# Turned weights split by TensorE, codes in fewer operations, and second counts taken early

## What is computed

```python
h = jnp.maximum(_layernorm(x, axis=-1), 0.0)
# layer 0: for each edge (s, d): relu(concat(h[s], h[d]) @ W0.T + b0), summed at s
x = x + _L0_gnn_ref(h, edge_index_t, 1250, L0_gnn_W, L0_gnn_b)
h = jnp.maximum(_layernorm(x, axis=-1), 0.0)
# layer 1: (h @ W1.T)[s] * edge_weight, summed at d, then out >= 0 ? out : alpha * out
x = x + _L1_gnn_ref(h, edge_index, edge_weight, 1250, L1_gnn_W, L1_gnn_alpha)
```

## Time and profile before

| | us |
|---|---|
| median of three runs | 1033.83 (1033.64 to 1035.51) |
| the profiled execution | 1024.19 |
| its span, first to last instruction | 1022.5 |
| TensorE, VectorE, ScalarE, GpSimd busy | 962.6, 889.8, 776.2, 663.5 |

### The profile page before, as it was taken

One profiled execution on the slowest core, in us unless ns is written; L12 is line 12 of the kernel. 1 busy time (PEld: TensorE's weight loads), 2 busy tenths in 40 slices (PEclk: granted clock), 3 DMA queues, 4 the chain that ended last, 5 costly groups with the idle time before them and its releaser, 6 DMA issues.

```text
span 1022.5 us, 20099 instructions
## 1 busy us (share of the span) xinstructions
PE 962.6 (94%) x4679; PEld 769.9 (75%) x4680; DVE 889.8 (87%) x1753; ACT 776.2 (76%) x1648; POOL 663.5 (65%) x942
## 2 busy tenths in 40 slices
PE   5389999999989999999999999999999999989998
PEld 4177778776758887888887888888888787878776
DVE  7989999898769999999999999999999788883444
ACT  6668788787868888888888888888888777764210
POOL 3788878786567777777777777777777755540000
PEclk9999999899979999999999999999999999999999
DMA  8000000000111111111111111111111000010011
GB/s 219 1 4 2 3 3 3 4 2 3 17 53 43 44 41 40 41 44 42 44 40 40 43 42 42 43 40 40 43 42 45 30 27 29 30 42 1 20 41 41
DMA packets 34384, 35.09 MB, mean 34 GB/s; under 512 B 6129, under 2 KB 30556, under 8 KB 34337
## 3 DMA queue, kind: packets, MB, share of 16 engines
q1 hardware_dynamic: 29636, 33.89, 10.8%
q0 software_dynamic: 4416, 0.30, 1.6%
q10 hardware_dynamic: 284, 0.33, 0.1%
HBM read 30.92 MB, written 3.29 MB: 33 GB/s over the span
## 4 chain that ended last, share of the span: by engine, by line
PE 68%; DVE 2%; ACT 1%; issue 0%; POOL 0%; POOLq 0%
PE node_ps L1127 8%; PE edge_ps L1166 8%; PE edge_ps L1172 8%; PE edge_ps L1171 7%; PE edge_ps L1167 7%; PE node_ps L1128 7%; PE m_ps L1138 4%; PE psum L1270 3%; PE psum L1272 3%; PE psum L1271 3%; PE m_ps L1252 1%; PE edge_ps L1230 1%; PE edge_ps L1231 1%; PE edge_ps L1227 1%; PE edge_ps L1222 1%; PE edge_ps L1226 1%
## 5 line engine op out<-in xcount | busy, mean ns | idle before, releaser
L1359 ACT ACTIVATE msg_hi<-edge_ps 128x512 fp32r<-128x512 f32 x332 | 198.0, 596 | 59.3 <-PE edge_ps L1172 59.3
L1083 POOL TENSOR_TENSOR M<-M,pair_w 125x125 f32 x332 | 161.2, 485 | 124.3 <-DVE pair_w L1506 94.6
L1520 DVE SCALAR_TENSOR_TENSOR msg_lo<-edge_ps,msg_hi 128x512 fp32r<-128x512 f32 x332 | 224.2, 684 | 17.1 <-ACT msg_hi L1359 12.3
L409 POOL DMA_INDIRECT edge_table<-fields,row_no x136 | 175.2, 1288 | 54.7 <-issue 46.4
L812 ACT ACTIVATE lane_piece<-hot_lane,fields 125x128 fp32r<-125x128 bf16 x498 | 155.8, 391 | 41.6 <-DVE hot_lane L495 41.4
L698 PE MATMUL psum<-hot_tile,lane_piece 125*128 125x384 f32 x582 | 147.2, 375 | 20.6 <-ACT lane_piece L812 19.5
L1067 POOL TENSOR_TENSOR hot_w<-hot_d,weight_l 128x252 fp32r<-128x252 bf16 x166 | 141.6, 853 | 0.0
L698 PEld LDWEIGHTS psum<-hot_tile,lane_piece 125*128 125x128 f32 x582 | 106.1, 197 | 42.1 <-ACT lane_piece L812 25.9
L1127 PE MATMUL node_ps<-msg_hi,hot_s 128*125 128x512 f32 x332 | 134.8, 406 | 0.0
L1166 PE MATMUL edge_ps<-b_hi,turned_d 125*128 x332 | 132.5, 399 | 0.9 <-ACT turned_d L1343 0.7
L1172 PE MATMUL edge_ps<-a_lo,turned_s 125*128 x332 | 131.5, 396 | 0.0
(11 more groups left out here) (256 smaller groups left out, 2062.6 us busy)
## 6 DMA issues: line engine op xcount, KB each, us to landing
spread<-edge_rows SPq DMA_DIRECT2D x190, 125.0 KB
out_dram<-result SPq DMA_DIRECT2D x10, 224.0 KB
edge_table<-fields,row_no POOLq DMA_INDIRECT x136, 2.6
w_in<-in_L_gnn_W_dram SPq DMA_DIRECT2D x1, 2048.0 KB, 11.7
S<-in_x_dram SPq DMA_DIRECT2D x1, 1792.0 KB
w_in<-in_L_gnn_W_dram SPq DMA_DIRECT2D x1, 1024.0 KB, 5.3
S<-in_x_dram SPq DMA_DIRECT2D x1, 448.0 KB
edge_table<-zeros SPq DMA_DIRECT2D x1, 384.0 KB, 15.5
```

What stands on the lines that cost most here:

```text
L409: pool.indirect_dma_start(table_dram[:, :], bass.IndirectOffsetOnAxis(ap=row_no[:, c:c + 1], axis=0), fields[:, c, 0:TABLE_FIELDS], None). ...
L1083: pool.tensor_tensor(part, part, pair_w[h][:, j, 0, 0:BN], ALU.add).then_inc(m_added, 1)
L1359: act.activation(msg_hi[j][:], edge_ps[j][:], ACT.Relu).then_inc(hi_ready, 1)
L1520: dve.scalar_tensor_tensor(out=msg_lo[j][:], in0=edge_ps[j][:], scalar=0.0, in1=msg_hi[j][:].bitcast(F32), op0=ALU.max, op1=ALU.subtract). ...
```

## The change

TensorE: `turn_w` is now a plain matmul with the identity as moving operand; each group of four opens with `start` and leaves the result to be added to. A new `low_w(i)` subtracts the rounded weights (`minus_ident` times `w0T[0]`) in the same PSUM bank, and ScalarE copies what is left as `w0T[1]`. `w0T_full` and GpSimd's eight subtractions are gone, as is the semaphore `w_full`; `w_low`, `ones_row_r` and `mix_bases` are new. The weights go in four pairs: two ahead of and around the column of bases, two behind the 15 prefixes and ahead of the first column. No transposing stands before the totals any more.

Counts of the second chunk are taken directly behind those of the first, in banks 0 and 2, and copied by ScalarE in two operations after the second pair of weights. VectorE makes the sixth block of `hot` before it waits for the totals, the mix bases before the scan, and leaves `base_up` to ScalarE. The codes are computed on one plane of 330 columns, without the operation over both planes. GpSimd's three `fields` operations wait for the codes instead of the base rows.

The core of the diff (blank lines and most context left out):

```diff
@@ -237,7 +236,10 @@
             HALF = CHUNK // 2
-            count_ps = psum[0:NBLK, 4:6, 0:HALF * NBLK]
+            def count_ps(k):
+                return [psum[0:NBLK, bank, 0:HALF * NBLK] for bank in ((0, 2) if k == 1 else (4, 5))]
             turn_ps = psum[:, 2, 0:KC * BN].rearrange("p (c n) -> p c n", c=KC)
@@ -367,7 +371,7 @@
-                    pool.tensor_copy(ones_r[:], ones[0:2, :]).then_inc(w_lo, 1)
+                    pool.tensor_copy(ones_r[:], ones[0:2, :]).then_inc(ones_row_r, 1)
                     own(pool.memset(all_one, 1.0))
@@ -378,17 +382,12 @@
-                    pool.wait_ge(base_rows, 2)
+                    pool.wait_ge(code_ready, 1)
                     pool.wait_ge(weight_in, 16)
...
                                        ALU.subtract).then_inc(fields_ready, 1)
-                    for i in range(2 * KC):
-                        pool.wait_ge(w_full, i + 1)
-                        pool.tensor_tensor(w0T[1][:, i, :], w0T_full[i][:], w0T[0][:, i, :].bitcast(F32),
-                                           ALU.subtract).then_inc(w_lo, 1)
@@ -542,6 +541,7 @@
                                       by_col[:].unsqueeze(1).to_broadcast(shape), ALU.mult).then_inc(spread_done, 1)
+                    hot_of_block(0, 5)
                     dve.tensor_copy(iota_h[:], iota[:, 0:P])
@@ -581,27 +581,25 @@
                     own(dve.tensor_reduce(counts[:, :, 0], own_base.rearrange("p s d -> p d s"), AX.X, ALU.add))
+                    own(dve.tensor_tensor(own_mix[:], base_p.rearrange("p (s q) k -> p s q k", s=NBLK)[0:NBLK, :, :, 1],
+                                          ident[0:NBLK, 0:NBLK].unsqueeze(2).to_broadcast([NBLK, NBLK, NBP]), ALU.mult))
+                    dve.tensor_reduce(mix_at[:], own_mix.rearrange("p s q -> p q s"), AX.X, ALU.add).then_inc(mix_bases, 1)
                     dve.wait_ge(consts, 5)
                     bases(0)
-                    own(dve.tensor_tensor(own_mix[:], base_p.rearrange("p (s q) k -> p s q k", s=NBLK)[0:NBLK, :, :, 1],
-                                          ident[0:NBLK, 0:NBLK].unsqueeze(2).to_broadcast([NBLK, NBLK, NBP]), ALU.mult))
-                    own(dve.tensor_reduce(mix_at[:], own_mix.rearrange("p s q -> p q s"), AX.X, ALU.add))
-                    dve.tensor_scalar(base_up.rearrange("s (q k) c -> s q (k c)", k=2),
-                                      mix_at[:].unsqueeze(2).to_broadcast([NBLK, NBP, 2 * CHUNK]), -float(MID_TILE), UPPER,
-                                      ALU.add, ALU.mult).then_inc(upper_row, 1)
-                    for s in range(5, NBLK):
+                    for s in range(6, NBLK):
                         hot_of_block(0, s)
-                    own(dve.scalar_tensor_tensor(out=local[:], in0=blk[:], scalar=-float(BN), in1=node_f[:],
+                    upper_bits = local[:, 0, :]
+                    own(dve.scalar_tensor_tensor(out=upper_bits, in0=node_f[:, 0, :], scalar=float(TILE), in1=node_f[:, 1, :],
                                                  op0=ALU.mult, op1=ALU.add))
-                    own(dve.scalar_tensor_tensor(out=local[:, 0, :], in0=local[:, 0, :], scalar=float(TILE),
-                                                 in1=local[:, 1, :], op0=ALU.mult, op1=ALU.add))
-                    own(dve.scalar_tensor_tensor(out=local[:, 0, :], in0=blk[:, 1, :], scalar=-UPPER / 2, in1=local[:, 0, :],
+                    own(dve.scalar_tensor_tensor(out=upper_bits, in0=blk[:, 0, :], scalar=-float(BN * TILE), in1=upper_bits,
                                                  op0=ALU.mult, op1=ALU.add))
-                    own(dve.scalar_tensor_tensor(out=local[:, 0, :], in0=pair_of, scalar=UPPER, in1=local[:, 0, :],
+                    own(dve.scalar_tensor_tensor(out=upper_bits, in0=blk[:, 1, :], scalar=-(UPPER / 2 + BN), in1=upper_bits,
                                                  op0=ALU.mult, op1=ALU.add))
-                    dve.tensor_scalar(fields[:].bitcast(I32)[:, :, CODE_AT], local[:, 0, :], float(SHIFT_S * TILE + 1) - UPPER,
+                    own(dve.scalar_tensor_tensor(out=upper_bits, in0=pair_of, scalar=UPPER, in1=upper_bits,
+                                                 op0=ALU.mult, op1=ALU.add))
+                    dve.tensor_scalar(fields[:].bitcast(I32)[:, :, CODE_AT], upper_bits, float(SHIFT_S * TILE + 1) - UPPER,
                                       65536.0, ALU.add, ALU.mult).then_inc(code_ready, 1)
@@ -664,11 +662,11 @@
                         for c in cols:
-                            if c == 0 and k > 0:
+                            if c == 0 and k > 1:
...
                             at = k * CHUNK + c
-                            mm = pe.matmul(count_ps[:, c // HALF, (c % HALF) * NBLK:(c % HALF + 1) * NBLK],
+                            mm = pe.matmul(count_ps(k)[c // HALF][:, (c % HALF) * NBLK:(c % HALF + 1) * NBLK],
                                            dig_s[:, :, at], dig_d[:, :, at], start=True, stop=True)
@@ -700,11 +698,25 @@
                     def turn_w(i):
                         if i >= 2:
-                            pe.wait_ge(w_full, i - 1)
+                            pe.wait_ge(w_lo, i - 1)
                         for o in range(KC):
-                            mm = pe.transpose(psum[:, 6 + i % 2, o * P:(o + 1) * P], w_in[:, o, i * P:(i + 1) * P], ident[:])
+                            mm = pe.matmul(psum[:, 6 + i % 2, o * P:(o + 1) * P], w_in[:, o, i * P:(i + 1) * P], ident[:],
+                                           start=(o == 0), stop=(o == KC - 1), skip_group_check=True)
                         mm.then_inc(w_ps, 1)
+                    def low_w(i):
+                        pe.wait_ge(w_hi, i + 1)
+                        pe.matmul(psum[:, 6 + i % 2, :], minus_ident[:], w0T[0][:, i, :], start=False, stop=True,
+                                  skip_group_check=True).then_inc(w_low, 1)
+                    def weights(pair):
+                        for i in (2 * pair, 2 * pair + 1):
+                            turn_w(i)
+                        for i in (2 * pair, 2 * pair + 1):
+                            low_w(i)
@@ -719,7 +731,8 @@
                             if b == 0 and m == 0:
-                                pe.wait_ge(w_lo, 2 * KC + 1)
+                                pe.wait_ge(w_lo, 2 * KC)
+                                pe.wait_ge(ones_row_r, 1)
                                 pe.wait_ge(bias_in, 32)
@@ -746,20 +759,26 @@
                     mm.then_inc(hist_done, 1)
-                    pe.wait_ge(w_loaded, 16)
-                    turn_w(0)
                     pe.wait_ge(spread_done, 1)
...
                     count(0, range(CHUNK))
-                    for i in range(1, 2 * KC):
-                        turn_w(i)
+                    count(1, range(CHUNK))
+                    pe.wait_ge(w_loaded, 16)
+                    pe.wait_ge(act_own, 2)
+                    weights(0)
...
                     pe.matmul(base_col_ps, tile_base[0:1, :], ones[0:1, 0:1], start=True, stop=True).then_inc(base_col, 1)
+                    weights(1)
                     for g in range(NPICK):
                         prefix(0, g)
+                    weights(2)
+                    weights(3)
                     pe.wait_ge(base_out, 1)
+                    pe.wait_ge(count_out, 2)
@@ -775,8 +794,6 @@
                                         low(b, m)
-                            if k == 0 and i < 3:
-                                count(1, range(CHUNK // 3 * i, CHUNK // 3 * (i + 1)))
                             part = i - last + COUNT_BACK
@@ -798,8 +815,14 @@
                             act.wait_ge(carried, k)
+                        if k == 1:
+                            for h in range(2):
+                                ins = act.copy(counts[:, :, 1 + h * HALF:1 + (h + 1) * HALF],
+                                               count_ps(k)[h].rearrange("s (c d) -> s d c", d=NBLK))
+                            ins.then_inc(count_out, 1)
+                            return
                         act.copy(counts[:, :, 1:CHUNK + 1].rearrange("s d (h c) -> s d h c", h=2),
-                                 count_ps.rearrange("s h (c d) -> s d h c", d=NBLK)).then_inc(count_out, 1)
+                                 psum[0:NBLK, 4:6, 0:HALF * NBLK].rearrange("s h (c d) -> s d h c", d=NBLK)).then_inc(count_out, 1)
@@ -849,31 +872,39 @@
-                    def turned_weights(i):
-                        act.wait_ge(w_ps, i + 1)
-                        act.copy(w0T[0][:, i, :], psum[:, 6 + i % 2, :])
-                        act.copy(w0T_full[i][:], psum[:, 6 + i % 2, :]).then_inc(w_full, 1)
+                    def turned_weights(pair):
+                        for i in (2 * pair, 2 * pair + 1):
+                            act.wait_ge(w_ps, i + 1)
+                            act.copy(w0T[0][:, i, :], psum[:, 6 + i % 2, :]).then_inc(w_hi, 1)
+                        for i in (2 * pair, 2 * pair + 1):
```

(16 more changed lines are left out.)

5 lines of the change are left out of this document (3 added, 2 removed).

## The result

| | kernel before | changed kernel |
|---|---|---|
| median, 17 runs each | 1032.28 (1027.84 to 1036.9) | 1023.22 (1015.37 to 1031.86) |
| profiled execution | 1024.19 | 1019.37 |
| its span | 1022.5 | 1017.6 |

The ratio is 0.9912, with a 95% interval of 0.989 to 0.9934: **9.1 us faster, 6.8 to 11.4**. More runs also moved the median of before, from 1033.83 to 1032.28. The medians are of all 17 runs each; three of the changed kernel (1031.62, 1031.70 and 1031.86), over 1.5% above its fastest, are counted as slow and left out of the ratio, and without them its median would be 1021.73.

A forecast was written before the change was run, and what follows sets the result against it. VectorE's own path was taken to set the stretch before the edge stage. Low clock 3.9 + 3.1 - 1.7 = 5.3 us, high 5.0 + 3.1 = 8.1; 6.5 taken: 1033.83 - 6.5 = 1027.3 us, range 1024.2 to 1031.7.

The forecast's parts named there:

- Earlier start of the bases: VectorE ahead of the codes: totals free of transposes, line 552 at 15.6 instead of 15.87, last hot block about 25.6 instead of 27.39.
- The codes: VectorE just before the picks: 2.5 us instead of 6.3 with GpSimd quiet, so picks could begin at 28.05.
- A turn: One weight turned on TensorE by plain fp32 matmuls: 8 x 0.23 = 1.82 us.
- TensorE ahead of the picks: Counts and two pairs of turns precede the first prefix: picks at about 29.8, 3.9 us won, 5.0 if the clock rises.
- Second counts: In the first columns: VectorE's 3.10 us wait for the second chunk's counts goes, 3.1 us won.
- ScalarE late: Weight copies ahead of column 0's pieces: first piece about 52.9, 1.7 us taken back at low clock, nothing at high.
- the high clock: Case of TensorE's clock rising during the dense turns, given one half: 5.0 + 3.1 = 8.1 us won, against 5.3 at low.
- the carrying over: Last step: gain taken from the profiled 1024.19, the median's 9.6 us above it added unchanged: 1033.83 - 6.5 = 1027.3.
- rival 4: It wins more: high clock and no catching up, 8.7 us, 1025.1, called the limit of VectorE's own path; chance 0.06.
- ScalarE as the bound of the chunk: Rival for the whole first chunk: 4 us taken back instead of 1.7, 3 us won, 1030.8; chance 0.16.
- rival 2: A turn on TensorE so dear that nothing is won or time is lost; chance 0.08, its edge near no change 0.05.
- The codes slowed by something else: Rival: VectorE's codes don't get faster, 3 us less ahead of the picks, 4 us won, 1029.8; chance 0.07.

The follow-up runs named there:

- e2: Kernel before, with one wait changed: GpSimd's fields operations and subtractions wait for the codes instead of the base rows; ratio to before 0.9981 (0.9956 to 1.0007).
- e4: Changed kernel with GpSimd's three fields operations waiting for the base rows again; ratio to before 0.9929 (0.9908 to 0.995).
- e3: Changed kernel with transposes in place of the plain matmuls, for times only as its remainders are wrong; ratio to before 0.9905 (0.987 to 0.994).
- e1: Kernel before, with the second chunk counted directly behind the first and copied by ScalarE ahead of the moments; ratio to before 0.997 (0.9948 to 0.9991).
- e8: Kernel before, with W0 sent behind the second part of x so that it lands late; ratio to before 1.0108 (1.0082 to 1.0134).
- e9: Changed kernel, with W0 sent behind the second part of x so that it lands late; ratio to before 1.0 (0.9973 to 1.0027).
- e7: Kernel before, with totals and first counts taken ahead of the first transposes and the wait for W0; ratio to before 0.9985 (0.9964 to 1.0006).
- e10: Changed kernel with turns 6 and 7 in PSUM banks 0 and 2, so four banks serve the last four turns; ratio to before 0.9906 (0.9874 to 0.9937).
- e5: Changed kernel with every turn of the weights done twice; ratio to before 0.9963 (0.9941 to 0.9984).
- e11: Changed kernel with transposes and the remainders left to GpSimd, but behind the codes and fields; ratio to before 0.9924 (0.9897 to 0.9951).
- e6: Changed kernel with the last two pairs' subtractions and turns spread behind columns 1, 3 and 5; ratio to before 0.9975 (0.9954 to 0.9995).

## Where the prediction was right, and which step failed

**Earlier start of the bases**: line 552 at 15.67, forecast 15.6. Right, but see the load below. A reading on the way was wrong: the two matmuls of the totals ran from 15.04, their first weight load, to 15.83, so they took 0.79 and not 0.54. It did no harm, since they took 0.74 in the change (14.77 to 15.51) and VectorE came behind them.

**The codes**: 2.44 us, forecast 2.5, in operations of 0.48 to 0.50. Right, and e2 shows the cause with a single line. Each slows the other: in e4 GpSimd took 2.83 instead of 0.78 and VectorE 1.27 instead of 0.50. In the kernel before, line 385 on GpSimd lasted until 29.06 (3.80 us, 1.06 in the change), through the last `hot` blocks and the first operation of the codes and into the second (28.18 to 29.42). By what means they do so wasn't shown.

**A turn**: 1.82 us at the lower clock forecast, 1.9 measured. The 0.23 in this term is how long a weight load of the kernel before lasted, and no run shows it as the price of an instruction: at 0.50 both kinds of turn start their instructions 0.21 apart, with loads of 0.23 (e3) as with loads of 0.33 (the change). 8 x 0.21 is 1.7; the pair that took 3.72 is fourteen such steps, a first one of 0.32 and the 0.42 that its last instruction lasted. **TensorE ahead of the picks**: I had the picks at 29.8, or 5.0 us won if the clock rose. It rose: turns 2 and 3 took 2.05 us together at a granted clock of 1.00, where later pairs at 0.50 took 3.72 and 3.78. The picks were 5.88 earlier, 0.9 more than even that case had. The mis-sized term is the transfer of `base_up`: I had ScalarE write it from 24.6 to 25.3, it did from 24.08 to 24.83, and the first prefix began at 27.17, 2.3 behind it, not 2.8. And VectorE was ready at 27.80, not 28.05. After all, the codes were last, not TensorE.

**Second counts**: 3.1 forecast, 3.18 measured in the change, 3.2 by itself in e1. Right.

**ScalarE late**: first piece at 50.23, forecast 52.9 (49.4 with the high clock); taken back 2.05, forecast 1.7 or 0. Here the clock did *not* rise (turns 4 to 7 took 3.72 and 3.78 a pair), so one pair of four had it; the value in the middle was right for that, by luck as much as by reason. The mechanism, waits for placed columns from the sixth on, is there: 1.4 us.

The sum at the second slots was 6.5, the profiles say 6.95. The path was mis-sized by 0.45.

**The step that failed** is the carrying over: the sum was made against one profiled execution and subtracted from the median, as if that execution had the typical times of everything on the path. The prediction put 9.64 us between the profiled execution and the median of either kernel. Over the 17 runs each it was 8.09 for before and 3.85 for the changed kernel.

One thing on the path is shown: the profile of before had an early load of W0. The 0.70 us that VectorE waited for the totals I put down to one group of transposes, and didn't ask what had released those, though the trace of before says so (0.77 us for the load). That it was the load of W0, that its landing moves by up to 3 us (which one profile can't show), and that the change takes it off the path, is in no step of the prediction; rival 4 even called 8.7 the limit of VectorE's own path. It adds about 0.9: 6.95 + 0.9 = 7.8, inside 6.8 to 11.4. The mechanism is shown by e1, e8 and e9; its size in the normal runs is the estimate above, and e7 (1.6, -0.6 to 3.7) neither contradicts nor proves it.

The last 1.3 us up to 9.1 stay open. The clock in the column stage is the candidate. The profile of before had 6.8 us at 0.50 there, where the other four of its kind have 17 to 25; the changed kernel's profile had 6.8 as well, but its runs have a higher mean clock. The estimate above gives 2 us for that. It isn't shown that the change causes it, and no experiment held the clock fixed.

**The range** was too narrow at its lower end for a plainer reason too. I took 0.9 us for the uncertainty of the baseline, from three runs; seventeen spread over 9.1, and the median moved by 1.55. Against 1032.28, the same gains would have given 1022.7 as the lower end, and the measured 1023.22 would have been in.

**The rivals.** ScalarE as the bound of the chunk: it took back 2.05, not 4, and e10, which frees it, gains nothing visible. A turn so dear that nothing is won or time is lost, for which rival 2's chances of 0.08 and 0.05 stand: no run shows it. The plain turn took 1.9 us, and even the doubled one of e5, up to 3.1 us for one, doesn't end slower than before (0.9963), since the clock rose during its first pair. The codes slowed by something else: refuted by e2. Wins more: nearest to the outcome, but its reasons were no catching up at all, where 2.05 was taken back, and the high clock in both pairs, where one had it. That its number was nearest is luck.

**No better version** came out of it: e3, e10 and e11 are level with the change, e4, e5 and e6 are behind it.

## What to carry to other kernels

When a profile shows a short wait on the critical engine, follow it back through the releaser's own queue to a transfer, if there is one: a load's landing differs by microseconds from one execution to the next (11.4 to 14.4 us here), and one profile shows one draw of it. Taking the work that waits for a load off the front of an in-order queue can be worth more than its wait in that profile. When a forecast is carried from a profile to a median, ask which draws that profile holds: here its load and its clock were both good ones. If vector operations take twice their usual time or more (here 1.24 to 1.45 us instead of 0.50), look at what GpSimd does in the same microseconds, and move that, not the work of VectorE; and be wary of scattering handoffs between two engines through a stream in which both are busy: in the one kernel here that did, both waited.
